# First context attention of a two-layer Perceiver block: where the softmax is divided by its sums

## Chip, cores and metric

The kernel runs on one core of a Trainium2 chip. The metric is device time in microseconds. The kernel before took 872.7 us (median of 3 runs, 870.73 to 873.6).

## The reference, cut to what matters

The whole program is a stack of attention, recurrence and feed-forward parts on x of 16 batches, 64 rows each, width 256. The change is in its first part, cross attention from the normalised rows to a context of 256 rows a batch, with 16 heads of 16 columns:

```
v = (values @ Wv.T).reshape(N, -1, H, D)
k = (keys @ Wk.T).reshape(N, -1, H, D)
q = (queries @ Wq.T).reshape(N, -1, H, D)
energy = jnp.einsum('nqhd,nkhd->nhqk', q, k)
attn = jax.nn.softmax(energy / jnp.sqrt(jnp.float32(E)), axis=3)
out = jnp.einsum('nhql,nlhd->nqhd', attn, v).reshape(N, -1, H * D)
return out @ Wo.T + bo
```

values and keys are both the context ctx_1024. The result is added to x.

## The kernel before, in words

Each stage is a block in which every engine has its own program, in order; engines meet only by semaphores. The first attention is first_attention_stage, about 21 to 166 us of the span. It goes over the 16 batches n. The 16 heads of a batch lie in four banks r = 0 to 3 of PSUM (s_ps), each 128 rows (two heads by 64 queries) by KD = 2 parts by 256 context rows.

For each batch: TensorE makes the scores of all four banks (scores, L1324). VectorE takes the maximum of each bank (maxima, L1479). ScalarE takes the exponential of each bank in two instructions and gets the row sums with them in den (exps, L1417). TensorE turns each bank (transposes, L1333: "turning" below, T(n,r) for bank r) into one of three work banks w_ps that are used in a fixed rotation, written out in the list uses. VectorE copies the turned banks 0 to 2 to probT, ScalarE bank 3 (take_transposed, L1485 and L1424). TensorE multiplies them with the values (values, L1347) into o_ps.

Before, the probabilities are turned undivided. VectorE takes the reciprocals of all sums of the batch (reciprocals, L1491). GpSimd lays them out times a mask (spread_out, L1249), and TensorE multiplies that with a doubled identity (L1353, in values) so that the factors lie as the heads do. At odd n, heads() copies the factors from PSUM (L1495) and multiplies the heads by them (L1499). The output projection of a pair of batches t = n // 2 stands between T(n,1) and T(n,2) of the next even n (output, L1360), and add() adds it to X.

Between these lie the projections for batch n + 3: its keys (keys_of, L1282) after the scores of n + 1, its values (values_of, L1291) after the value product of n. ScalarE takes both to SBUF, the keys between exponentials 1 and 2, the values after exponential 3. For n = 5 and 9 there are also a turning of x and a query projection (query, L1311). GpSimd also makes the query halves (queries, L1239: two instructions for a pair of batches), adds the output bias to X (add_bias) and makes the inverse roots for the next stage's normalisation (following.root, L189 and L193). root at odd n waits for the moments, which VectorE makes in following.find_moments (L122, L184) in its turn of the same n. following.scale_row (L199) on VectorE stands at even n from 4 on.

TensorE's order for one n is written out: four turnings, with the output between T1 and T2 at even n; scores of n + 1; keys of n + 3; value and spreading products of n; values of n + 3. There are no keys or values left to make from n = 13 on.

Of the kernel before, what the change touches and what calls it, by code (L numbers as in the profile page):

```python
# [13 lines left out]
P = 128  # L14
B = 16
# [1104 lines left out]
def first_attention_stage(nc, stage, X, eps, xnT, QT, par_q, half, twice, ident, x_d, ctxT_d, WqT, WkT, WvT, WoT, bo, firsts, constants, others, others_loaded, following):  # L1120
# [14 lines left out]
    with Scope(nc, stage) as sc:  # L1135
# [5 lines left out]
        negmax = [sc.sb(f"negmax{j}", [P, 4, KD]) for j in range(2)]  # L1141
        prob = [sc.sb(f"prob{j}", [P, 4, KD, S]) for j in range(2)]
        probT = [sc.sb(f"probT{j}", [P, 4, KD, 2, P]) for j in range(2)]
        den = [sc.sb(f"den{j}", [P, KD, 4]) for j in range(2)]
        rden = [sc.sb(f"rden{j}", [P, KD, 4]) for j in range(2)]
        spread = [sc.sb(f"spread{j}", [P, KD, 4, 2 * HD]) for j in range(2)]
        factor = sc.sb("factor", [P, 2 * KD, T])
        headsT = sc.sb("headsT", [P, 2 * KD, T])
        s_ps = [sc.ps(f"s_ps{r}", [P, KD, S]) for r in range(4)]
        w_ps = [sc.ps(f"w_ps{i}", [P, 512]) for i in range(3)]  # L1150
        o_ps = sc.ps("o_ps", [P, 2, 2 * KD, T])
        ctx_in = [sc.sem(f"ctx_in{j}") for j in range(NB)]
        (zeroed, k_mm, k_ready, v_mm, v_ready, q_ready, s_mm, max_ready, exp_done, pt_mm, pt_dve, pt_act, pv_mm, rden_ready, spread_ready, factor_ready, heads_ready, out_mm, x_added) = (sc.sem(n) for n in (
            "zeroed", "k_mm", "k_ready", "v_mm", "v_ready", "q_ready", "s_mm", "max_ready", "exp_done", "pt_mm", "pt_dve", "pt_act", "pv_mm",
            "rden_ready", "spread_ready", "factor_ready", "heads_ready", "out_mm", "x_added"))
        turned, turned_taken, query_mm, query_taken, bias_added, constant = (sc.sem(n) for n in ("turned", "turned_taken", "query_mm", "query_taken", "bias_added", "constant"))
        x_in = [sc.sem(f"x_in{g}") for g in range(CH)]
        wk_in, wv_in, turn_in, wq_in, rest_in = (sc.sem(n) for n in ("wk_in", "wv_in", "turn_in", "wq_in", "rest_in"))
        on_act = (3,)
        on_dve = tuple(r for r in range(4) if r not in on_act)  # L1160

        def loaded(n):
# [41 lines left out]
        with sc.block() as block:  # L1204
# [27 lines left out]
            @block.gpsimd  # L1232
            def _(pool):
                def queries(t):
                    pool.wait_ge(query_taken, ONE + t // 2 + 1)
                    if t >= 2:
                        pool.wait_ge(s_mm, ONE + 4 * (2 * t - 2))
                    for e in range(2):
                        nc.gpsimd.tensor_scalar(qpair[t % 2][:, :, :, e, :], QT[:, :, t * P:(t + 1) * P].rearrange("p m (j q) -> p m j q", j=2), par_q[:, e:e + 1], None, ALU.mult).then_inc(q_ready, 1)  # L1239

                def add_bias(t):
                    pool.wait_ge(normed.scaled, ONE + t + 1)
                    nc.gpsimd.tensor_tensor(X[:, t, :], X[:, t, :], bo[:, :], ALU.add).then_inc(bias_added, 1)

                def spread_out(n):
                    pool.wait_ge(rden_ready, ONE + n + 1)
                    if n >= 2:
                        pool.wait_ge(pv_mm, ONE + n - 1)
                    nc.gpsimd.tensor_tensor(spread[n % 2][:, :, :, :].rearrange("p m r d -> p (m r) d"), rden[n % 2][:, :, :].rearrange("p m r -> p (m r)").unsqueeze(2).to_broadcast([P, 4 * KD, 2 * HD]),  # L1249
                                            half[:, :].unsqueeze(1).to_broadcast([P, 4 * KD, 2 * HD]), ALU.mult).then_inc(spread_ready, 1)  # L1250

                following.prepare(pool)
                for j in range(AHEAD):
                    nc.gpsimd.memset(vals[j][:, :, :, :, :], 0.0).then_inc(zeroed, 1)
                pool.wait_ge(rest_in, ONE + 16 * len(firsts["rest"]))
                queries(0)
                queries(1)
                for n in range(B):
                    if n % 2 == 0:
                        if 2 <= n // 2 + 1 < NT:  # L1260
                            queries(n // 2 + 1)
                        add_bias(n // 2)
                    spread_out(n)
                    if n % 2 == 1 and n >= 3:
                        following.root(pool, n // 2 - 1, n // 2)

            @block.tensor
            def _(pe):
# [58 lines left out]

                def transposes(n, r):
                    acc = work_bank((n, r))
                    pe.wait_ge(exp_done, ONE + 4 * n + r + 1)  # L1330
                    for m in range(KD):
                        for c in range(2):
                            mm = nc.tensor.transpose(acc[:, (2 * m + c) * P:(2 * m + c + 1) * P], prob[n % 2][:, r, m, c * P:(c + 1) * P], ident[:, :])  # L1333
                    mm.then_inc(pt_mm, 1)

                def values(n):
                    t, j = n // 2, n % 2
                    pe.wait_ge(v_ready, ONE + 2 * n + 2)
                    if j == 0 and t >= 1:
                        pe.wait_ge(heads_ready, ONE + t)  # L1340
                    for r in (2, 3):
                        pe.wait_ge(*transposed(n, r))
                    for m in range(KD):
                        for e in range(2):
                            for c in range(2):
                                for r in range(4):
                                    nc.tensor.matmul(o_ps[32 * r:32 * r + 32, 0, 2 * m + j, :], vals[n % AHEAD][:, e, c, 4 * m + r, :],  # L1347
                                                     probT[n % 2][:, r, m, c, e * T:(e + 1) * T], start=(e == c == 0), stop=(e == c == 1))
                    if n == 0:
                        pe.wait_ge(rest_in, ONE + 16 * len(firsts["rest"]))  # L1350
                    pe.wait_ge(spread_ready, ONE + n + 1)
                    for m in range(KD):
                        mm = nc.tensor.matmul(o_ps[:, 1, 2 * m + j, :], spread[n % 2][:, m, :, :], twice[:, :], start=True, stop=True)  # L1353
                    mm.then_inc(pv_mm, 1)

                def output(t):
                    pe.wait_ge(heads_ready, ONE + t + 1)
                    acc = work_bank(("out", t))
                    for k in range(KD):
# [13 lines left out]
                for n in range(B):  # L1373
                    ahead = TURNED_BESIDE.get(n)
                    for r in range(4):
# [4 lines left out]
                            query(1)  # L1380
                        if r == 1 and ahead is not None:
                            turn(ahead)
                    if n + 1 < B:
                        scores(n + 1)
                    if ahead is not None:
                        query(ahead)
                    if n + AHEAD < B:
# [7 lines left out]
            def _(act):  # L1395
# [16 lines left out]
                def exps(n, r):  # L1412
# [1 line left out]
                    if n >= 2:  # L1414
                        act.wait_ge(pt_mm, ONE + 4 * (n - 2) + r + 1)
                    for m in range(KD):
                        ins = nc.scalar.activation(prob[n % 2][:, r, m, :], s_ps[r][:, m, :], ACT.Exp, bias=negmax[n % 2][:, r, m:m + 1], accum_out=den[n % 2][:, m, r:r + 1])  # L1417
                    ins.then_inc(exp_done, 1)

                def take_transposed(n, r):  # L1420
# [53 lines left out]
            def _(dve):  # L1474
# [9 lines left out]
                        dve.wait_ge(pv_mm, ONE + n - 1)  # L1484
                    nc.vector.tensor_copy(probT[n % 2][:, r, :, :, :], bank((n, r))[:, :].rearrange("p (m c q) -> p m c q", m=KD, c=2)).then_inc(pt_dve, 1)  # L1485

                def reciprocals(n):
                    dve.wait_ge(exp_done, ONE + 4 * n + 4)
                    if n >= 2:
                        dve.wait_ge(spread_ready, ONE + n - 1)  # L1490
                    nc.vector.reciprocal(rden[n % 2][:, :, :], den[n % 2][:, :, :]).then_inc(rden_ready, 1)  # L1491

                def heads(t):
                    dve.wait_ge(pv_mm, ONE + 2 * t + 2)
                    nc.vector.tensor_copy(factor[:, :, :], o_ps[:, 1, :, :]).then_inc(factor_ready, 1)  # L1495
                    dve.wait_ge(factor_ready, ONE + t + 1)
                    if t >= 1:
                        dve.wait_ge(out_mm, ONE + t)
                    nc.vector.tensor_tensor(headsT[:, :, :], o_ps[:, 0, :, :], factor[:, :, :], ALU.mult).then_inc(heads_ready, 1)  # L1499

                def add(t):
                    dve.wait_ge(out_mm, ONE + t + 1)
# [18 lines left out]
                normed.scale(dve, NT - 1)  # L1521
                for r in range(4):
                    maxima(0, r)
                for n in range(B):
                    for r in range(4):
                        if r == 3:
                            reciprocals(n)
                        if r not in on_act:
                            take_transposed(n, r)
                        if r == 2 and n % 2 == 0 and n > 0:  # L1530
                            add(n // 2 - 1)
                    if n + 1 < B:
                        for r in range(4):
                            maxima(n + 1, r)
                    if n % 2 == 1 and n >= 3:
                        dve.wait_ge(x_added, ONE + n // 2)
                        following.find_moments(dve, n // 2 - 1)
                    if n % 2 == 1:
                        heads(n // 2)
                    if n % 2 == 0 and n >= 4:  # L1540
                        following.scale_row(dve, n // 2 - 2)
                add(NT - 1)


# [1638 lines left out]
```

## Time and profile before

| | us |
|---|---|
| median of 3 runs | 872.7 |
| profiled execution, its own time | 875.52 |
| its span | 873.7 |
| TensorE busy in the span | 754.0 (86%) |
| VectorE busy | 564.5 (65%) |
| ScalarE busy | 416.0 (48%) |
| GpSimd busy | 328.6 (38%) |
| mean granted clock of TensorE | 0.936 of full |

PE is TensorE's matmul, PEld its weight load, DVE is VectorE, ACT ScalarE, POOL GpSimd. Times in the rows are us from the start of the span. The span is somewhat shorter than the execution's own time.

### The profile page before, as it was taken

The page shows a single profiled execution, that of the slowest core. Times are in us where ns is not written, and L with a number is a line of the kernel's source. Part 1 is how long each engine was busy: PE and PEld are TensorE (multiplying, and loading weights), DVE is VectorE, ACT ScalarE, POOL GpSimd, SP SyncE. Part 2 cuts the span into 40 slices and gives each one's busy share as a digit, 9 for nine tenths or more (in the row PEclk, how much of TensorE's full clock was granted, in tenths as well). Part 3 has the DMA queues.
Part 4 walks back from the last instruction along what each step waited for, and adds up shares of the span by engine and source line. Part 5 has one row for each costly group of instructions (what it writes and reads, how often), then busy time and mean ns, then how long its engine had stood idle before and what let it go on. Part 6 is the DMA issues. An engine that isn't in the chain of part 4 may idle for free. (4 is left out here: it accounts for less than half of the span.)

```text
span 873.7 us, 19103 instructions
## 1 busy us (share of the span) xinstructions
PE 754.0 (86%) x7000; PEld 504.6 (58%) x7000; DVE 564.5 (65%) x1234; ACT 416.0 (48%) x1253; POOL 328.6 (38%) x424
## 2 busy tenths in 40 slices
PE   6999999798899999968787399999378888868996
PEld 5788887544333333345465388888257776456334
DVE  3565556536799999976797433232478887567474
ACT  3755656462655665235463100000267884645572
POOL 2222222127477887731253450100554553334001
PEclk9999999998799999988998599999679999979999
DMA  8111710000020000000001046542456420000001
GB/s 268 37 42 54 266 26 2 2 1 1 24 74 1 1 1 1 0 2 0 2 3 50 25 138 192 175 158 73 132 170 194 124 75 2 1 3 3 0 1 50
DMA packets 44893, 51.79 MB, mean 59 GB/s; under 512 B 7072, under 2 KB 40832, under 8 KB 44544
## 3 DMA queue, kind: packets, MB, share of 16 engines
q1 hardware_dynamic: 40256, 43.48, 16.0%
q0 software_dynamic: 1536, 4.20, 1.6%
q10 hardware_dynamic: 3008, 2.88, 0.9%
q8 instruction: 57, 0.93, 0.4%
q14 instruction: 36, 0.29, 0.1%
HBM read 45.31 MB, written 5.24 MB: 58 GB/s over the span
## 5 line engine op out<-in xcount | busy, mean ns | idle before, releaser
L1008 PE MATMUL r_u_ps<-r_t_in,l_same_head 128*128 128x512 f32 x124 | 69.6, 643 | 1.1
L1807 ACT ACTIVATE a_prob<-a_s_ps,a_negmax 128x256 f32<-128x256 f32 x128 | 58.7, 482 | 22.3 <-DVE a_negmax L1843 21.7
L976 POOL TENSOR_TENSOR r_q_in<-r_state,rec_q 128x512 f32<-128x512 f32 x62 | 68.1, 1098 | 0.0
L1417 ACT ACTIVATE a_prob<-a_s_ps,a_negmax 128x256 f32<-128x256 f32 x128 | 59.1, 487 | 17.8 <-DVE a_negmax L1479 17.8
L2436 PE MATMUL m_h_ps<-m_rowsT,l_w 128*128 128x256 f32 x256 | 57.8, 386 | 0.0
L1485 DVE COPY a_probT<-a_w_ps 128x512 f32<-128x512 f32 x48 | 31.4, 687 | 37.2 <-PE a_w_ps L1333 37.0
L2447 PE MATMUL m_y_ps<-l_w,m_hidden 128*128 128x256 f32 x240 | 53.9, 379 | 0.0
L2436 PEld LDWEIGHTS m_h_ps<-m_rowsT,l_w 128*128 128x128 f32 x256 | 49.7, 195 | 7.0
L1843 DVE TENSOR_REDUCE a_negmax<-a_s_ps 128x2 f32<-128x512 f32 x64 | 41.3, 684 | 18.4 <-PE a_s_ps L1723 14.0
L966 POOL TENSOR_TENSOR r_faded<-r_state,rec_both 128x256 f32<-128x256 f32 x62 | 39.8, 642 | 33.5 <-DVE r_state L945 33.5
L2479 ACT ACTIVATE m_rowsT<-m_xt_ps,l_B_s,l_B_g 128x256 f32<-128x256 f32 x16 | 8.2, 559 | 92.4 <-PE m_xt_ps L2424 85.7
L2341 DVE TENSOR_SCALAR m_hidden<-m_h_ps,l_b 128x256 f32<-128x256 f32 x64 | 28.0, 480 | 36.9 <-PE m_h_ps L2436 36.1
L1479 DVE TENSOR_REDUCE a_negmax<-a_s_ps 128x2 f32<-128x512 f32 x64 | 39.8, 684 | 16.2 <-PE a_s_ps L1324 16.2
L2447 PEld LDWEIGHTS m_y_ps<-l_w,m_hidden 128*128 128x128 f32 x240 | 45.1, 190 | 5.9
L936 DVE TENSOR_TENSOR r_update<-r_u_ps,rec_k 128x512 f32<-128x512 f32 x64 | 44.3, 693 | 1.6 <-PE r_u_ps L1002 1.5
L932 DVE TENSOR_TENSOR r_t_in<-r_state,r_par_ps 128x512 f32<-128x512 f32 x62 | 42.6, 687 | 3.2
L2080 POOL TENSOR_TENSOR a_prob<-a_prob,a_rden 128x512 f32<-128x512 f32 x32 | 32.3, 1041 | 30.6 <-DVE a_rden L2149 30.6
L1249 POOL TENSOR_TENSOR a_spread<-a_rden,all_half 128x256 f32<-128x256 f32 x16 | 9.8, 614 | 89.2 <-DVE a_rden L1491 89.2
L1732 PE MATMUL a_w_ps<-all_ident,a_prob 128*128 128x128 f32 x256 | 38.9, 299 | 3.9 <-DVE a_probT L1849 1.7
L1282 PE MATMUL a_w_ps<-a_ctxT,l_A_WkT 128*128 128x256 f32 x128 | 33.4, 406 | 7.1 <-DMA l_A_WkT<-in_A_WkT 6.2
L2365 POOL DMA_INDIRECT m_rows<-routed_rows,m_token x16 | 15.5, 967 | 63.5 <-PE m_xt_ps L2424 42.7
L1732 PEld LDWEIGHTS a_w_ps<-all_ident,a_prob 128*128 128x128 f32 x256 | 31.5, 155 | 12.3 <-issue 7.9
(404 smaller groups left out, 1861.7 us busy)
## 6 DMA issues: line engine op xcount, KB each, us to landing
l_w<-in_B_w SPq DMA_DIRECT2D x16, 1024.0 KB, 5.8
a_ctxT<-in_ctxT SPq DMA_DIRECT2D x31, 256.0 KB, 2.9
a_ctx<-in_ctx SPq DMA_DIRECT2D x16, 256.0 KB, 2.8
expert_out<-m_y ACTq DMA_DIRECT2D x7, 256.0 KB, 5.7
all_X<-in_x SPq DMA_DIRECT2D x4, 256.0 KB, 5.5
l_b<-in_B_b SPq DMA_DIRECT2D x1, 1024.0 KB, 6.0
own_rows<-n_rows SPq DMA_DIRECT2D x2, 512.0 KB, 3.0
all_xnT<-own_rows SPq DMA_DIRECT2D x1, 1024.0 KB, 5.3
```

What stands on the lines that cost most here:

```text
L932: nc.vector.tensor_tensor(t_in[m][:, :, :, :], twice(state[n % 2][m]), a, ALU.mult).then_inc(t_ready[m], 1)
L936: nc.vector.tensor_tensor(update[m][:, :, :, :], u_ps[m][:, :, :, :], steps("k", 2 * n, 2, m), ALU.mult).then_inc(upd_ready[m], 1)
L966: nc.gpsimd.tensor_tensor(faded[m][:, :, :], state[n % 2][m][:, :, :], f, ALU.mult).then_inc(faded_ready[m], 1)
L976: ins = nc.gpsimd.tensor_tensor(q_in[i % 2][m][:, :, :, :], twice(state[i % 2][m]), steps("q", 2 * i - 1, 2, m), ALU.mult)
L1008: nc.tensor.matmul(u_ps[m][:, :, :, :], same_head[:, :], t_in[m][:, :, :, :], start=False, stop=True).then_inc(u_mm[m], 1)
L1417: ins = nc.scalar.activation(prob[n % 2][:, r, m, :], s_ps[r][:, m, :], ACT.Exp, bias=negmax[n % 2][:, r, m:m + 1], accum_out=den[n % 2][: ...
L1479: nc.vector.tensor_reduce(negmax[n % 2][:, r, :], s_ps[r][:, :, :], AX.X, ALU.max, negate=True).then_inc(max_ready, 1)
L1732: mm = nc.tensor.transpose(acc[:, (2 * m + c) * P:(2 * m + c + 1) * P], prob[n % 2][:, r, m, c * P:(c + 1) * P], ident[:, :])
L1807: ins = nc.scalar.activation(prob[n % 2][:, r, m, :], s_ps[r][:, m, :], ACT.Exp, bias=negmax[n % 2][:, r, m:m + 1], accum_out=den[n % 2][: ...
L1843: nc.vector.tensor_reduce(negmax[n % 2][:, r, :], s_ps[r][:, :, :], AX.X, ALU.max, negate=True).then_inc(max_ready, 1)
L2436: mm = nc.tensor.matmul(h_ps[i][:, f, :], w1[j][:, k, (2 * i + f) * P:(2 * i + f + 1) * P], rowsT[j][:, k, :], start=(k == 0), stop=(k == ...
L2447: mm = nc.tensor.matmul(y_bank(e, slice(c, c + 1))[:, 0, :], hidden[j][:, f, c * P:(c + 1) * P], w2[j][:, f, :], start=(f == 0), stop=(f = ...
```

## The change

The probabilities are divided before they are turned. GpSimd multiplies each bank of prob, in place, by the reciprocals of its row sums (normalise, four instructions a batch); the turnings wait for that in place of the exponential. The spreading on GpSimd, the spreading product on TensorE, and the factor copy and product in heads() are dropped; heads() is one copy. VectorE takes the reciprocals bank by bank. TensorE's scores of n + 1 move ahead of T(n,3). ScalarE now copies turned bank 2, VectorE 0, 1 and 3. VectorE's order is written anew.

```diff
-        on_act = (3,)
+        on_act = (2,)
...
-                def spread_out(n):
-                    pool.wait_ge(rden_ready, ONE + n + 1)
...
+                def normalise(n, r):
+                    pool.wait_ge(rden_ready, ONE + 4 * n + r + 1)
+                    nc.gpsimd.tensor_tensor(prob[n % 2][:, r, :, :], prob[n % 2][:, r, :, :], rden[n % 2][:, r, :].unsqueeze(2).to_broadcast([P, KD, S]), ALU.mult).then_inc(prob_ready, 1)
...
                 for n in range(B):
+                    for r in range(4):
+                        normalise(n, r)
                     if n % 2 == 0:
                         if 2 <= n // 2 + 1 < NT:
                             queries(n // 2 + 1)
                         add_bias(n // 2)
-                    spread_out(n)
                     if n % 2 == 1 and n >= 3:
                         following.root(pool, n // 2 - 1, n // 2)
...
                 def transposes(n, r):
                     acc = work_bank((n, r))
-                    pe.wait_ge(exp_done, ONE + 4 * n + r + 1)
+                    pe.wait_ge(prob_ready, ONE + 4 * n + r + 1)
...
-                    pe.wait_ge(spread_ready, ONE + n + 1)
-                    for m in range(KD):
-                        mm = nc.tensor.matmul(o_ps[:, 1, 2 * m + j, :], spread[n % 2][:, m, :, :], twice[:, :], start=True, stop=True)
...
-                    if n + 1 < B:
-                        scores(n + 1)
+                        if r == 2 and n + 1 < B:
+                            scores(n + 1)
...
-                def reciprocals(n):
-                    dve.wait_ge(exp_done, ONE + 4 * n + 4)
+                def reciprocals(n, r):
+                    dve.wait_ge(exp_done, ONE + 4 * n + r + 1)
...
                 def heads(t):
                     dve.wait_ge(pv_mm, ONE + 2 * t + 2)
-                    nc.vector.tensor_copy(factor[:, :, :], o_ps[:, 1, :, :]).then_inc(factor_ready, 1)
-                    dve.wait_ge(factor_ready, ONE + t + 1)
                     if t >= 1:
                         dve.wait_ge(out_mm, ONE + t)
-                    nc.vector.tensor_tensor(headsT[:, :, :], o_ps[:, 0, :, :], factor[:, :, :], ALU.mult).then_inc(heads_ready, 1)
+                    nc.vector.tensor_copy(headsT[:, :, :], o_ps[:, :, :]).then_inc(heads_ready, 1)
...
+                for r in range(4):
+                    reciprocals(0, r)
                 for n in range(B):
...
+                    take_transposed(n, 0)
+                    take_transposed(n, 1)
+                    if n % 2 == 0 and n > 0:
+                        add(n // 2 - 1)
                     if n + 1 < B:
...
+                        maxima(n + 1, 0)
+                        maxima(n + 1, 1)
+                    take_transposed(n, 3)
+                    if n + 1 < B:
+                        reciprocals(n + 1, 0)
+                        maxima(n + 1, 2)
+                        reciprocals(n + 1, 1)
+                        maxima(n + 1, 3)
+                    if n % 2 == 1:
+                        heads(n // 2)
+                    if n + 1 < B:
+                        reciprocals(n + 1, 2)
                     if n % 2 == 1 and n >= 3:
                         dve.wait_ge(x_added, ONE + n // 2)
                         following.find_moments(dve, n // 2 - 1)
-                    if n % 2 == 1:
-                        heads(n // 2)
                     if n % 2 == 0 and n >= 4:
                         following.scale_row(dve, n // 2 - 2)
+                    if n + 1 < B:
+                        reciprocals(n + 1, 3)
```

## Rows read from the trace of the kernel before

**Rows 1.** Busy time by stretch: engine busy us, granted clock, DMA share, GB/s
```profile
29.73:148.10 118.37, 117.99 (x1557) 96.37 (x1556) 70.07 (x138) 73.62 (x264) 26.81 (x41) 1.00 0.24 76
```

**Rows 2.** Timeline, TensorE, 84 to 94 us: start, length, instructions
```profile
84.78 1.15 PE L1324 MATMUL a_s_ps<-a_keysT,a_qpair 32*128 32x256 f32 x16
...
87.78 1.10 PE L1347 MATMUL a_o_ps<-a_probT,a_vals 128*32 128x64 f32 x64
88.81 0.66 PE L1353 MATMUL a_o_ps<-all_twice,a_spread 128*128 128x64 f32 x4
89.30 1.95 PE L1291 MATMUL a_w_ps<-l_A_WvT,a_ctxT 128*128 128x256 f32 x8
91.08 2.04 PE L1333 MATMUL a_w_ps<-all_ident,a_prob 128*128 128x128 f32 x16
93.06 1.15 PE L1324 MATMUL a_s_ps<-a_keysT,a_qpair 32*128 32x256 f32 x16
```

**Rows 3.** Timeline, TensorE, the scores one frame later
```profile
102.27 1.15 PE L1324 MATMUL a_s_ps<-a_keysT,a_qpair 32*128 32x256 f32 x16
```

**Rows 4.** Timeline, ScalarE, same frame: sum reads that end each bank's exponential
```profile
87.49 0.20 ACT L1417 ACTIVATION_READ_ACCUMULATOR a_prob<-a_s_ps,a_negmax 128x1 f32 x1
...
88.38 0.21 ACT L1417 ACTIVATION_READ_ACCUMULATOR a_prob<-a_s_ps,a_negmax 128x1 f32 x1
...
89.76 0.24 ACT L1417 ACTIVATION_READ_ACCUMULATOR a_prob<-a_s_ps,a_negmax 128x1 f32 x1
...
90.66 0.25 ACT L1417 ACTIVATION_READ_ACCUMULATOR a_prob<-a_s_ps,a_negmax 128x1 f32 x1
```

**Rows 5.** Timeline, VectorE, same frame: the four maxima
```profile
85.94 2.49 DVE L1479 TENSOR_REDUCE a_negmax<-a_s_ps 128x2 f32<-128x512 f32 x4 [0.36 <-PE a_s_ps L1324]
```

**Rows 6.** Timeline, VectorE, the moments for the next stage at n = 7
```profile
96.62 0.42 DVE L122 BATCH_NORM_STATS2 n_x_parts<-all_X 128x6 f32<-128x256 f32 x1
97.07 0.18 DVE L184 BATCH_NORM_AGGREGATE n_x_meanvar<-n_x_parts 128x2 f32<-128x6 f32 x1
```

**Rows 7.** Timeline, GpSimd, root at n = 7 and the queries behind it
```profile
97.33 0.19 POOL L189 TENSOR_TENSOR n_x_std<-n_x_meanvar,all_eps 128x1 f32<-128x1 f32 x1 [2.92 <-DVE n_x_meanvar L184]
...
98.16 1.83 POOL L1239 TENSOR_SCALAR a_qpair<-all_QT,all_par 128x256 f32<-128x256 f32 x2
```

**Rows 8.** Timeline, a later attention: reciprocal, normalising, turning
```profile
436.35 0.19 DVE L2149 RECIPROCAL a_rden<-a_den 128x8 f32<-128x8 f32 x1
...
436.63 4.04 POOL L2080 TENSOR_TENSOR a_prob<-a_prob,a_rden 128x512 f32<-128x512 f32 x4 [1.92 <-DVE a_rden L2149]
...
437.72 3.75 PE L2034 MATMUL a_pt_ps<-all_ident,a_prob 128*128 128x128 f32 x16 [0.40 <-POOL a_prob L2080]
```

**Rows 9.** Timeline, TensorE, the frame with a query projection
```profile
73.60 1.15 PE L1324 MATMUL a_s_ps<-a_keysT,a_qpair 32*128 32x256 f32 x16
74.94 1.97 PE L1311 MATMUL a_w_ps<-all_xnT,l_A_WqT 128*128 128x256 f32 x8 [0.19 <-ACT all_xnT L1428]
```

**Rows 10.** Timeline, TensorE, batch 0: T(0,1) and the scores of batch 1
```profile
26.47 0.63 PE L1333 MATMUL a_w_ps<-all_ident,a_prob 128*128 128x128 f32 x4 [0.88 <-ACT a_prob L1417]
...
29.73 1.15 PE L1324 MATMUL a_s_ps<-a_keysT,a_qpair 32*128 32x256 f32 x16
```

**Rows 11.** Timeline, the last batches: scores of 14 and 15, last heads
```profile
148.10 1.15 PE L1324 MATMUL a_s_ps<-a_keysT,a_qpair 32*128 32x256 f32 x16
...
155.06 1.15 PE L1324 MATMUL a_s_ps<-a_keysT,a_qpair 32*128 32x256 f32 x16
...
164.44 0.42 DVE L1499 TENSOR_TENSOR a_headsT<-a_o_ps,a_factor 128x256 f32<-128x256 f32 x1
```

**Rows 12.** Scaling of rows (min/median/max ns, all of the line), and two of them beside GpSimd
```profile
L142 DVE TENSOR_SCALAR a_x_rows<-all_X,a_x_meanvar,a_x_rstd x8: 383/410/1115, 7.8 to 13.6; 128x256 f32<-128x256 f32 x8
...
9.82 1.87 DVE L142 TENSOR_SCALAR a_x_rows<-all_X,a_x_meanvar,a_x_rstd 128x256 f32<-128x256 f32 x2
...
8.67 2.87 POOL L1254 MEMSET a_vals<- 128x1024 f32 x3
```

More of the change, by code:

```diff
@@ L1143, in first_attention_stage @@
         probT = [sc.sb(f"probT{j}", [P, 4, KD, 2, P]) for j in range(2)]
[L1144 to L1147, printed above, removed]
+        den = [sc.sb(f"den{j}", [P, 4, KD]) for j in range(2)]
+        rden = [sc.sb(f"rden{j}", [P, 4, KD]) for j in range(2)]
         headsT = sc.sb("headsT", [P, 2 * KD, T])
@@ L1150, in first_attention_stage @@
         w_ps = [sc.ps(f"w_ps{i}", [P, 512]) for i in range(3)]
-        o_ps = sc.ps("o_ps", [P, 2, 2 * KD, T])
+        o_ps = sc.ps("o_ps", [P, 2 * KD, T])
         ctx_in = [sc.sem(f"ctx_in{j}") for j in range(NB)]
-        (zeroed, k_mm, k_ready, v_mm, v_ready, q_ready, s_mm, max_ready, exp_done, pt_mm, pt_dve, pt_act, pv_mm, rden_ready, spread_ready, factor_ready, heads_ready, out_mm, x_added) = (sc.sem(n) for n in (
+        (zeroed, k_mm, k_ready, v_mm, v_ready, q_ready, s_mm, max_ready, exp_done, pt_mm, pt_dve, pt_act, pv_mm, rden_ready, prob_ready, heads_ready, out_mm, x_added) = (sc.sem(n) for n in (
             "zeroed", "k_mm", "k_ready", "v_mm", "v_ready", "q_ready", "s_mm", "max_ready", "exp_done", "pt_mm", "pt_dve", "pt_act", "pv_mm",
-            "rden_ready", "spread_ready", "factor_ready", "heads_ready", "out_mm", "x_added"))
+            "rden_ready", "prob_ready", "heads_ready", "out_mm", "x_added"))
         turned, turned_taken, query_mm, query_taken, bias_added, constant = (sc.sem(n) for n in ("turned", "turned_taken", "query_mm", "query_taken", "bias_added", "constant"))
@@ L1243, in add_bias @@
                     nc.gpsimd.tensor_tensor(X[:, t, :], X[:, t, :], bo[:, :], ALU.add).then_inc(bias_added, 1)
-                def spread_out(n):
-                    pool.wait_ge(rden_ready, ONE + n + 1)
[L1247 to L1250, printed above, removed]
+                def normalise(n, r):
+                    pool.wait_ge(rden_ready, ONE + 4 * n + r + 1)
+                    nc.gpsimd.tensor_tensor(prob[n % 2][:, r, :, :], prob[n % 2][:, r, :, :], rden[n % 2][:, r, :].unsqueeze(2).to_broadcast([P, KD, S]), ALU.mult).then_inc(prob_ready, 1)
                 following.prepare(pool)
@@ L1346, in values @@
                                 for r in range(4):
-                                    nc.tensor.matmul(o_ps[32 * r:32 * r + 32, 0, 2 * m + j, :], vals[n % AHEAD][:, e, c, 4 * m + r, :],
+                                    mm = nc.tensor.matmul(o_ps[32 * r:32 * r + 32, 2 * m + j, :], vals[n % AHEAD][:, e, c, 4 * m + r, :],
                                                      probT[n % 2][:, r, m, c, e * T:(e + 1) * T], start=(e == c == 0), stop=(e == c == 1))
-                    if n == 0:
-                        pe.wait_ge(rest_in, ONE + 16 * len(firsts["rest"]))
-                    pe.wait_ge(spread_ready, ONE + n + 1)
-                    for m in range(KD):
-                        mm = nc.tensor.matmul(o_ps[:, 1, 2 * m + j, :], spread[n % 2][:, m, :, :], twice[:, :], start=True, stop=True)
                     mm.then_inc(pv_mm, 1)
                 def output(t):
+                    if t == 0:
+                        pe.wait_ge(rest_in, ONE + 16 * len(firsts["rest"]))
                     pe.wait_ge(heads_ready, ONE + t + 1)
@@ L1416, in exps @@
                     for m in range(KD):
-                        ins = nc.scalar.activation(prob[n % 2][:, r, m, :], s_ps[r][:, m, :], ACT.Exp, bias=negmax[n % 2][:, r, m:m + 1], accum_out=den[n % 2][:, m, r:r + 1])
+                        ins = nc.scalar.activation(prob[n % 2][:, r, m, :], s_ps[r][:, m, :], ACT.Exp, bias=negmax[n % 2][:, r, m:m + 1], accum_out=den[n % 2][:, r, m:m + 1])
                     ins.then_inc(exp_done, 1)
@@ L1485, in take_transposed @@
                     nc.vector.tensor_copy(probT[n % 2][:, r, :, :, :], bank((n, r))[:, :].rearrange("p (m c q) -> p m c q", m=KD, c=2)).then_inc(pt_dve, 1)
-                def reciprocals(n):
-                    dve.wait_ge(exp_done, ONE + 4 * n + 4)
+                def reciprocals(n, r):
+                    dve.wait_ge(exp_done, ONE + 4 * n + r + 1)
                     if n >= 2:
-                        dve.wait_ge(spread_ready, ONE + n - 1)
-                    nc.vector.reciprocal(rden[n % 2][:, :, :], den[n % 2][:, :, :]).then_inc(rden_ready, 1)
+                        dve.wait_ge(prob_ready, ONE + 4 * (n - 2) + r + 1)
+                    nc.vector.reciprocal(rden[n % 2][:, r, :], den[n % 2][:, r, :]).then_inc(rden_ready, 1)
                 def heads(t):
                     dve.wait_ge(pv_mm, ONE + 2 * t + 2)
-                    nc.vector.tensor_copy(factor[:, :, :], o_ps[:, 1, :, :]).then_inc(factor_ready, 1)
-                    dve.wait_ge(factor_ready, ONE + t + 1)
                     if t >= 1:
                         dve.wait_ge(out_mm, ONE + t)
-                    nc.vector.tensor_tensor(headsT[:, :, :], o_ps[:, 0, :, :], factor[:, :, :], ALU.mult).then_inc(heads_ready, 1)
+                    nc.vector.tensor_copy(headsT[:, :, :], o_ps[:, :, :]).then_inc(heads_ready, 1)
                 def add(t):
@@ L1523, in _ @@
                     maxima(0, r)
+                for r in range(4):
+                    reciprocals(0, r)
                 for n in range(B):
[L1525 to L1531, printed above, removed]
-                    if n + 1 < B:
-                        for r in range(4):
-                            maxima(n + 1, r)
+                    take_transposed(n, 0)
+                    take_transposed(n, 1)
+                    if n % 2 == 0 and n > 0:
+                        add(n // 2 - 1)
+                    if n + 1 < B:
+                        maxima(n + 1, 0)
[10 more added lines that the diff above has]
+                        reciprocals(n + 1, 2)
                     if n % 2 == 1 and n >= 3:
```

## The prediction

> **What bounds the kernel now.** The table of busy time by stretch comes first. In the 118.37 us from the scores of batch 1 to those of batch 14 TensorE is busy 117.99 us, at a granted clock of 1.00, while VectorE has 70.07, ScalarE 73.62 and GpSimd 26.81 [rows 1]. So in this stretch TensorE's instruction order is the clock of everything, and GpSimd is nearly free. The timeline of TensorE then gives the beat. I call the time from the start of one batch's scores to the start of the next a frame, and give times from its start as +x. A frame without an output projection is 84.78 to 93.06, 8.28 us [rows 2]; one with it is 93.06 to 102.27, 9.21 us [rows 2, 3]. Inside a frame: scores, keys of n+3, value product (+3.00), spreading product (+4.03), values of n+3 (+4.52), the four turnings (+6.30), next scores (+8.28). Third, when the other engines are done with the batch whose scores opened the frame: the four maxima start at +1.16 and take 2.49 [rows 5]; the exponentials of its four banks end at +2.91, +3.81, +5.22 and +6.13 [rows 4].
>
> **What goes.** The spreading product holds TensorE from 88.81 to 89.30: 0.49 us a batch [rows 2]. Since TensorE is the bound, each frame that gets no new wait is 0.49 shorter: 7.79, and 8.72 with output. The GpSimd spreading, the copy of the factors and the product in heads() are off the path in those frames; heads() keeps one copy, 0.42 for this shape [rows 11].
>
> **What comes.** GpSimd normalises 64 tiles of 128x512, in place, between exponential and turning. The stretch of before has no such instruction, the later attention does: four in 4.04, each 1.04 long and 1.00 from the last, the first 0.09 after its reciprocal (436.54 to 436.63), and TensorE starts 0.05 after the first is done (437.67 to 437.72) [rows 8]. Bounds for ours, with two broadcasts of 256 where that has eight of 64: not below a maximum over the same 512 columns on VectorE, 2.49 / 4 = 0.62 [rows 5]; not above 1.83, what GpSimd needs for 2 x 256 columns of the query halves [rows 7]. I take 1.04 and a pace of 1.00, the same operation on the same columns. A reciprocal is 0.19 [rows 8]; the new ones are four a batch, of two numbers.
>
> An even frame (n even, opened by scores n+1) then runs like this. T(n,3) now comes after the scores, so the value product starts at +3.00 + 0.49 = +3.49. The first reciprocal is at about +3.1, GpSimd starts at +3.3 (it may end the queries and the bias of this batch first, so at the latest near +3.7), and tiles are ready at about +4.4, +5.5, +6.5, +7.6. TensorE wants them at +6.30, +6.8, +7.3 and, after the next scores, +8.9. Each is a microsecond or so early: no wait, and the 0.49 stands. Keys and values keep their three banks; what turning waits for there is as far behind it as before.
>
> **An odd frame from n = 3 on is another matter**, and this is the term that decides. At the end of GpSimd's turn for odd n stands following.root(), which waits for moments that VectorE makes in the same turn. GpSimd takes its instructions in order, so normalise(n+1, 0) is queued behind that wait. In the profile root waits already today: 2.92 us, until the aggregate ends at 97.25, then runs 97.33 to 98.16, 0.83 with its second step, and only then come the queries [rows 6, 7]; nothing urgent was behind it. Now VectorE's order puts in front of the moments both heads(), which waits for the value product, and the reciprocal of bank 2, which waits for its exponential:
> - value product +3.49 to +4.6 (1.10 long [rows 2]); heads +4.7 to +5.1;
> - exponential 2 ends +5.22 [rows 4], reciprocal 2 to +5.4;
> - moments 0.63 from first start to last end [rows 6]: +6.03;
> - root +6.12 to +6.95 [rows 7]; tile 0 to +7.98, so T(n+1,0) at +8.03 and T(n+1,1) at +9.03, against +6.30 wanted;
> - then 0.5, output 0.93, T(n+1,2) 0.5 (its tile is ready by +10.0): next scores at +10.96.
> Against 9.21 before, that is +1.75. Three frames are such (n = 3, 7, 11). For n = 5 and 9 a query projection stands between, which moves keys and value product: the old frame is 73.60 to 84.78 = 11.18, less 9.21 and its own wait of 0.19 is 1.78 [rows 2, 3, 9]. Heads ends at +6.8, reciprocal 2 (its exponential now waits behind the keys, to about +6.8) at +7.05, moments +7.7, root +8.6, T0 +9.7, T1 +10.7, next scores +12.6: +1.44 each.
>
> **The two ends.** Batch 0: T(0,1) started at 26.47 behind its exponential [rows 10]; reciprocal, tile and hand-overs put about 0.3 + 1.04 + 0.05 in front, less the 0.14 it waited anyway: +1.27, and with T(0,3) moved behind the scores (-0.49) the scores of batch 1, 29.73, come 0.8 late. Frame 13 has no keys or values to fill TensorE: before it was 148.10 to 155.06 = 6.96 [rows 11]. Now heads +5.15, reciprocal 2 +5.3, moments +5.93, root +6.85, T0 +7.93, T1 +8.93, output, T2, scores of 15 at +10.85: +3.9. Frame 14: tiles ready at +4.3, 5.4, 6.4, 7.35; T3 ends +8.0, its copy +8.75, value product +9.9, heads done +10.4 against 155.06 to 164.86 = 9.80 [rows 11]: +0.6.
>
> A contention at the same place: scale_row() is SBUF to SBUF on VectorE. Two such instructions took 1.87 us at 9.82, beside GpSimd's fills (8.67 to 11.54), where the median of one is 410 ns and the longest 1115 [rows 12]. With normalising beside it in every even turn, reciprocal 3 can come a tile (1.04) late; tile 3 has 8.9 - 7.6 = 1.3 to spare, so only frame 14 pays, half a tile on average: +0.5. The Trainium skill, page "SBUF — State Buffer", section "SBUF: two separate sides", says VectorE in a 2-port mode and GpSimd hold one port pair by exclusive lock and the loser blocks for the whole instruction. Rows 12 agree. By that rule the price is the one above; without it the sum would be 0.5 less.
>
> **The sum.** Start +0.8; eight free frames (n = 0, 1, 2, 4, 6, 8, 10, 12) 8 x -0.49 = -3.9; n = 3, 7, 11: 3 x 1.75 = +5.25; n = 5, 9: 2 x 1.44 = +2.9; frame 13 +3.9; frame 14 +0.6 and +0.5. Together +10.0. The profiled execution took 875.52 (span 873.7), so its counterpart is 885.5. It stands 2.8 above the median of 872.7, so the forecast is 872.7 + 10.0 = 882.7.
>
> **Rivals.**
> - Faster: GpSimd's root does not hold the tiles up (the moments are there in time), so TensorE stays the bound. The thirteen frames before frame 13 would give 13 x -0.49 = -6.4, start +0.8, frame 13 +0.3 (T0 at +4.4 behind a tile), frame 14 +1.1: -4.2, so 868.5. For it: rows 1 and the slack of the even frames. Against it: root's wait is in the profile, and the new order makes it later, not earlier. Chance 0.07.
> - A shorter tile: at the lower bound of 0.62 a stalled frame has T0 at +7.6, then TensorE runs on, scores at +10.0, 0.95 less in each of six: +4.3, so 877. Chance 0.10.
> - GpSimd becomes the bound: with a tile near 1.83, four are 7.3 and queries come on top, more than a frame of 7.79. Both kinds of frame then follow GpSimd, about 2 us more in each of 16: 30 more, so about 912. Against it: the 1.04 of the same operation [rows 8]. Chance 0.03.
> - That the spreading product does not disappear from TensorE's bound, with its 0.49 refilled by an unseen wait in every frame (each reciprocal's semaphore): eight frames give nothing, +13.9, so 886.6. Chance 0.08.
> The likeliest keeps 0.72, with a range of its own of 879 to 886: half a microsecond of error in each of the six stalls is 3.
>
> **How the numbers follow.** A difference under 0.3% (2.6 us) can't be told from none. Faster takes the first rival, 0.07, and a sliver for errors in the stalls: 0.08. Same is 870.1 to 875.3, which needs the short tile and shorter stalls together: 0.05. Slower holds the rest, 0.87. The range reaches from the short tile, 876, a little beyond the refilled bound, 888; outside stay the faster case, the bound on GpSimd and the far ends of the rest, under 0.2.
>
> **What would show it.** Right: no spreading product; scores to scores 7.8 in even frames; in odd frames from 3 on GpSimd idle until the aggregate of n_x_meanvar, root behind it, TensorE idle some 1.7 before the first turning and 0.5 before the second, released by GpSimd's prob, and about 11.0 from scores to scores; busy share of TensorE down to about nine tenths there. Wrong: GpSimd's root waiting for nothing, or TensorE waiting for a tile in even frames too, or tiles far from 1.04.

## The result: 1.5% slower, and the profile after

The changed kernel took 883.92 us (median of 4, 882.72 to 884.62) against 871.72 for the kernel before, ratio 1.0154 (95% interval 1.0130 to 1.0178). Compared again later, side by side with two repaired kernels, it was 882.02 against 870.35, ratio 1.0133 (1.0101 to 1.0165). That is +11.7 to +12.2, where the forecast was +10.0.

Busy time by stretch, the changed kernel, from the scores of batch 1 to those of batch 14 (columns as in [rows 1]):

```profile
31.30:157.69 126.39, 116.90 (x1506) 93.18 (x1505) 73.10 (x170) 73.78 (x265) 71.86 (x80) 0.96 0.22 71
```

TensorE is busy 1.1 us less than before (116.90 against 117.99), in a stretch that is 8.0 longer, and it is now idle for 9.5 of it. Thirteen spreading products of 0.49 have gone from this stretch, so by itself that should have been 6.4 less; in a second profile of the same kernel (experiment 8) it is 6.1 less, 111.90 at a clock of 1.00. Here the mean clock is 0.96, so something beside idle time was lost. GpSimd went from 26.81 to 71.86.

The timeline of TensorE in the frame n = 7, the changed kernel, shows both losses (the same instructions as [rows 2, 3]):

```profile
96.46 1.15 PE L1320 MATMUL a_s_ps<-a_keysT,a_qpair 32*128 32x256 f32 x16
97.54 0.66 PE L1329 MATMUL a_w_ps<-all_ident,a_prob 128*128 128x128 f32 x4
98.03 1.89 PE L1278 MATMUL a_w_ps<-a_ctxT,l_A_WkT 128*128 128x256 f32 x8
99.85 1.10 PE L1343 MATMUL a_o_ps<-a_probT,a_vals 128*32 128x64 f32 x64
100.88 1.99 PE L1287 MATMUL a_w_ps<-l_A_WvT,a_ctxT 128*128 128x256 f32 x8
104.49 0.63 PE L1329 MATMUL a_w_ps<-all_ident,a_prob 128*128 128x128 f32 x4 [1.61 <-POOL a_prob L1245]
105.49 1.09 PE L1329 MATMUL a_w_ps<-all_ident,a_prob 128*128 128x128 f32 x4 [0.37 <-POOL a_prob L1245]
106.37 1.91 PE L1353 MATMUL a_w_ps<-l_A_WoT,a_headsT 128*128 128x256 f32 x4
108.07 1.01 PE L1329 MATMUL a_w_ps<-all_ident,a_prob 128*128 128x128 f32 x4
```

Up to the values of n + 3 every step is within 0.1 of where the forecast put it (value product +3.39, forecast +3.49). Then TensorE is idle 1.61 before the first turning and 0.37 before the second, both released by GpSimd's prob. The second turning, the output projection and the third turning are slow: the output takes 1.91, where the kernel before has, in the same frame:

```profile
100.37 1.10 PE L1360 MATMUL a_w_ps<-l_A_WoT,a_headsT 128*128 128x256 f32 x4
```

The same frame of the changed kernel on GpSimd and VectorE (timelines) gives the cause of the idle time:

```profile
99.43 0.15 DVE L1484 RECIPROCAL a_rden<-a_den 128x2 f32<-128x2 f32 x1
...
101.02 0.42 DVE L1490 COPY a_headsT<-a_o_ps 128x256 f32<-128x256 f32 x1
101.71 0.17 DVE L1484 RECIPROCAL a_rden<-a_den 128x2 f32<-128x2 f32 x1 [0.27 <-ACT a_prob L1410]
101.80 0.41 DVE L122 BATCH_NORM_STATS2 n_x_parts<-all_X 128x6 f32<-128x256 f32 x1
102.24 0.18 DVE L184 BATCH_NORM_AGGREGATE n_x_meanvar<-n_x_parts 128x2 f32<-128x6 f32 x1
```

```profile
102.50 0.19 POOL L189 TENSOR_TENSOR n_x_std<-n_x_meanvar,all_eps 128x1 f32<-128x1 f32 x1 [6.16 <-DVE n_x_meanvar L184]
102.77 0.57 POOL L193 TENSOR_TENSOR n_x_rstd<-n_x_std,n_x_minus_half 128x1 f32<-128x1 f32 x1
103.30 4.03 POOL L1245 TENSOR_TENSOR a_prob<-a_prob,a_rden 128x512 f32<-128x512 f32 x4
107.31 1.83 POOL L1237 TENSOR_SCALAR a_qpair<-all_QT,all_par 128x256 f32<-128x256 f32 x2
```

GpSimd stood 6.16 us in root, while the first reciprocal of the new batch was there from 99.58 (99.43 + 0.15) on. The moments ended at +5.96 of the frame (forecast +6.03), the first tile started at +6.84 (forecast +6.95). Granted clock over the slow products, the changed kernel:

```profile
106.37:108.07 1.70, 1.70 (x5) 1.24 (x5) 0.69 (x1) 0.00 (x0) 1.70 (x2) 0.50 1.03 399
```

0.50 is the lower of the two levels, 1.2 GHz. GpSimd and VectorE worked beside the output projection in the kernel before as well (at 100.37, GpSimd's bias from 99.95 to 100.67 and VectorE's copies from 100.00 to 101.29), at a clock of 1.00.

From scores to scores, us (before: two profiles that agree within 0.02; the changed kernel: the profile above, and a second one of the same kernel, the eighth experiment below):

| frame | before | forecast | profile shown | second profile |
|---|---|---|---|---|
| scores 0 to scores 1 | 8.08 | 8.9 | 10.54 | 8.87 |
| n = 0, 2, 6, 10, 12 | 8.28 | 7.79 | 7.75 | 7.75 |
| n = 4, 8 (8.88 before, a turning of x more) | 8.88 | 8.39 | 8.23 | 8.23 |
| n = 1 | 9.21 | 8.72 | 8.73 | 8.72 |
| n = 3, 7, 11 | 9.21 | 10.96 | 12.55 | 10.90 |
| n = 5, 9 | 11.18 | 12.6 | 12.40 | 12.40 |
| n = 13 | 6.96 | 10.85 | 12.21 | 12.22 |
| sum, scores 0 to scores 15 | 133.4 | 142.3 | 149.14 | 142.53 |

### The profile page after: what moved, and what is told of

The parts are those of the page before. It is cut to its first block and busy times, and to the rows that moved or that the text cites. A ratio compares the mean times of both kernels' runs of the same rounds, so it can differ in the third digit from the quotient of the medians.

```text
span 881.9 us, 19089 instructions
## 1 busy us (share of the span) xinstructions
PE 753.3 (85%) x6936; PEld 501.4 (57%) x6936; DVE 567.9 (64%) x1274; ACT 415.4 (47%) x1253; POOL 384.7 (44%) x472
## 5 line engine op out<-in xcount | busy, mean ns | idle before, releaser
L1245 POOL TENSOR_TENSOR a_prob<-a_prob,a_rden 128x512 f32<-128x512 f32 x64 | 65.4, 1047 | 27.6 <-DVE a_rden L1484 27.5
L1472 DVE TENSOR_REDUCE a_negmax<-a_s_ps 128x2 f32<-128x512 f32 x64 | 42.1, 682 | 27.4 <-PE a_s_ps L1320 27.4
L1329 PE MATMUL a_w_ps<-all_ident,a_prob 128*128 128x128 f32 x256 | 42.4, 301 | 16.1 <-POOL a_prob L1245 16.0
L1843 DVE TENSOR_REDUCE a_negmax<-a_s_ps 128x2 f32<-128x512 f32 x64 | 40.9, 681 | 11.9 <-PE a_s_ps L1723 11.9
L2080 POOL TENSOR_TENSOR a_prob<-a_prob,a_rden 128x512 f32<-128x512 f32 x32 | 32.3, 1042 | 31.4 <-DVE a_rden L2149 31.4
L1732 PE MATMUL a_w_ps<-all_ident,a_prob 128*128 128x128 f32 x256 | 38.4, 295 | 3.7 <-ACT a_prob L1807 2.4
```

Of the source, the lines that this page charges most:

```text
L1245: nc.gpsimd.tensor_tensor(prob[n % 2][:, r, :, :], prob[n % 2][:, r, :, :], rden[n % 2][:, r, :].unsqueeze(2).to_broadcast([P, KD, S]), AL ...
L1472: nc.vector.tensor_reduce(negmax[n % 2][:, r, :], s_ps[r][:, :, :], AX.X, ALU.max, negate=True).then_inc(max_ready, 1)
L1843: nc.vector.tensor_reduce(negmax[n % 2][:, r, :], s_ps[r][:, :, :], AX.X, ALU.max, negate=True).then_inc(max_ready, 1)
```

## The experiments

**1. Root later.** Only GpSimd's order is changed:

```diff
                     for r in range(4):
                         normalise(n, r)
+                    if n % 2 == 0 and n >= 4:
+                        following.root(pool, n // 2 - 2, n // 2 - 1)
...
-                    if n % 2 == 1 and n >= 3:
-                        following.root(pool, n // 2 - 1, n // 2)
+                following.root(pool, NT - 2, NT - 1)
```

> The changed kernel with one edit: GpSimd's root for the moments of turn n (odd) stands behind the four normalisings of n + 1, so no tile waits for the moments. Theory (the root in GpSimd's queue holds the tiles, and TensorE's slow products after the idle time follow from it): frames n = 3, 7, 11 go from 12.55 to about 8.75, n = 5 and 9 from 12.4 to about 10.7, frame 13 from 12.2 to about 7.5; together -19, so about 865. Rival (the normalising itself, its four hand-overs a batch, is what costs): frames stay within 1 us of the changed kernel, about 880 to 884.

Measured 863.99 against 869.29 for the kernel before: ratio 0.9935 (0.9914 to 0.9956), so it is faster than the kernel before and the changed kernel. Frames n = 3, 7, 11: 8.72; n = 5, 9: 10.45; 13: 7.25. The timeline of GpSimd, n = 3 to 4, has normalising first and root behind it:

```profile
58.74 2.04 POOL L1245 TENSOR_TENSOR a_prob<-a_prob,a_rden 128x512 f32<-128x512 f32 x2 [3.42 <-DVE a_rden L1485]
61.03 2.04 POOL L1245 TENSOR_TENSOR a_prob<-a_prob,a_rden 128x512 f32<-128x512 f32 x2 [0.26 <-DVE a_rden L1485]
63.03 0.19 POOL L189 TENSOR_TENSOR n_x_std<-n_x_meanvar,all_eps 128x1 f32<-128x1 f32 x1
```

The root's place in the queue is the cause. Normalising on GpSimd by itself costs the full frames nothing; the first and last ones keep a little (8.9 or 10.5 for 8.08, 7.25 for 6.96, and 10.5 for 9.8 from the last scores to the last heads).

**2. Moments first.** VectorE's find_moments moved ahead of heads() and reciprocal 2, a smaller dose of the same.

```diff
+                    if n % 2 == 1 and n >= 3:
+                        dve.wait_ge(x_added, ONE + n // 2)
+                        following.find_moments(dve, n // 2 - 1)
                     if n % 2 == 1:
                         heads(n // 2)
```

> The changed kernel with VectorE's moments moved ahead of heads() and of reciprocal 2, behind maximum 3; root stays where it is on GpSimd. Theory: the aggregate ends 0.75 earlier (+5.3 in place of +6.0), tile 0 as well, so TensorE's idle time before the first turning at n = 4, 8, 12 shrinks from 1.6 to about 0.9; with the granted clock falling as before that is 6 x -0.75 = -4.5, about 879.5; if it no longer falls at the shorter gap, another -1.3 in each of n = 3, 7, 11, about 875. Rival (the normalising itself costs): 884, no change.

Measured 874.9 (ratio 1.0051, 1.0027 to 1.0075), the lower of the two expected times. Timelines of GpSimd and TensorE, n = 3:

```profile
60.79 0.19 POOL L189 TENSOR_TENSOR n_x_std<-n_x_meanvar,all_eps 128x1 f32<-128x1 f32 x1 [5.47 <-DVE n_x_meanvar L184]
```

```profile
62.79 0.63 PE L1329 MATMUL a_w_ps<-all_ident,a_prob 128*128 128x128 f32 x4 [0.84 <-POOL a_prob L1245]
63.79 0.63 PE L1329 MATMUL a_w_ps<-all_ident,a_prob 128*128 128x128 f32 x4 [0.37 <-POOL a_prob L1245]
64.25 1.03 PE L1353 MATMUL a_w_ps<-l_A_WoT,a_headsT 128*128 128x256 f32 x4
```

Root starts 0.77 earlier and the idle time falls from 1.62 to 0.84, as expected; the output is back at 1.03, the frame 10.1. So in these frames what the moments gain is given back one for one (10.90 without the lower clock, less 0.78, is 10.12). At n = 5 and 9 the stall went altogether (10.45), more than the 0.75 expected. There heads() waits for a value product that comes a query projection later, so that the moments gain 2.3 by no longer standing behind it (they end at +5.17 of the frame n = 5, in the changed kernel at +7.47), and the idle time was only 1.41.

**3. Filler.** The stall stays; TensorE gets unread products (ident by WoT, 128x256, into a score bank already read) before the first turning of n = 4, 8, 12 and 14.

```diff
+                    if n in (4, 8, 12, 14):
+                        pe.wait_ge(exp_done, ONE + 4 * n + 1)
+                        for i in range(7 if n == 14 else 4):
+                            nc.tensor.matmul(s_ps[0][:, 0, :], ident[:, :], WoT[:, 0, :], start=True, stop=True)
```

> The changed kernel with the stall left in, but TensorE given products that nobody reads (128x256, four at n = 4, 8, 12 and seven at n = 14) ahead of the first turning. Theory (TensorE's granted clock falls to the lower level after the idle time, and the output projection and the third turning pay for it): frames n = 3, 7, 11 go from 12.55 to about 11.1 and frame 13 from 12.2 to about 11, together -5.4, about 878.5, with 4 output matmuls in 0.94 again in place of 1.9. Rival (those products are slow because GpSimd or VectorE is in their way): the frames stay at 12.5 or grow, 884 or more.

Median 880.65 (ratio 1.0131, 1.0104 to 1.0159): in time it can't be told from the changed kernel. In the profile the frames are 10.9 and frame 13 is 10.49. Timeline of TensorE, n = 3, whose scores start at 55.48 (55.53 in the changed kernel's first profile, frames within 0.05 until then):

```profile
61.73 1.89 PE L1371 MATMUL a_s_ps<-l_A_WoT,all_ident 128*128 128x256 f32 x8
63.53 0.63 PE L1329 MATMUL a_w_ps<-all_ident,a_prob 128*128 128x128 f32 x4
64.52 0.63 PE L1329 MATMUL a_w_ps<-all_ident,a_prob 128*128 128x128 f32 x4 [0.37 <-POOL a_prob L1245]
64.99 1.03 PE L1353 MATMUL a_w_ps<-l_A_WoT,a_headsT 128*128 128x256 f32 x4
```

GpSimd and VectorE are as busy as before, and the output takes 1.03: they were not in its way. Frame 13 is the firm part. In both profiles of the changed kernel, and in experiment 2, its output projection took 1.8 to 1.9 (experiment 8 has the lines); with the gap filled it takes 1.03 and the frame 1.7 less, 10.49 for 12.21:

```profile
161.78 1.03 PE L1353 MATMUL a_w_ps<-l_A_WoT,a_headsT 128*128 128x256 f32 x4
```

For n = 3, 7 and 11 this is one profile, and experiment 8 below shows what that is worth.

**4. No spreading.** The removed part alone, on the kernel before: no reciprocals, no spread_out, no spreading product, heads copied undivided.

```diff
-                    spread_out(n)
...
-                    pe.wait_ge(spread_ready, ONE + n + 1)
-                    for m in range(KD):
-                        mm = nc.tensor.matmul(o_ps[:, 1, 2 * m + j, :], spread[n % 2][:, m, :, :], twice[:, :], start=True, stop=True)
```

> The kernel before without the spreading on GpSimd, the spreading product, the reciprocals and the factors; the heads are copied undivided, so the division by the sums is left out of the first attention. It gives the price of the removed part alone. Theory (TensorE is the bound): 0.49 less in each of 13 frames and about 0.5 to 1 in the last two, -7.2, about 864.5. Rival (another wait takes the 0.49 up): 871 to 872.

Measured 862.95 (ratio 0.9913, 0.9881 to 0.9946). Timeline of TensorE; the values of n + 3 now follow the value product directly:

```profile
45.47 1.15 PE L1323 MATMUL a_s_ps<-a_keysT,a_qpair 32*128 32x256 f32 x16
...
48.47 1.10 PE L1346 MATMUL a_o_ps<-a_probT,a_vals 128*32 128x64 f32 x64
49.50 1.99 PE L1290 MATMUL a_w_ps<-l_A_WvT,a_ctxT 128*128 128x256 f32 x8
51.33 2.04 PE L1332 MATMUL a_w_ps<-all_ident,a_prob 128*128 128x128 f32 x16
53.30 1.15 PE L1323 MATMUL a_s_ps<-a_keysT,a_qpair 32*128 32x256 f32 x16
```

53.30 - 45.47 = 7.83 against 8.28: 0.45 a frame, nearly the whole 0.49. TensorE was the bound.

**5 and 10. Batch 0 mended.** Experiment 1 with reciprocal 0 between the maxima, and three unread products ahead of the first turning.

```diff
+                    if n == 0:
+                        pe.wait_ge(exp_done, ONE + 1)
+                        pe.wait_ge(rest_in, ONE + 16 * len(firsts["rest"]))
+                        for i in range(3):
+                            nc.tensor.matmul(s_ps[0][:, 0, :], ident[:, :], WoT[:, 0, :], start=True, stop=True)
```

> The kernel of the first experiment (root behind the next normalisings) with batch 0 mended too: reciprocal 0 between the maxima, and three unread products of 128x256 on TensorE ahead of the first turning, so that it isn't idle there. Theory (in batch 0 TensorE idles 1.5 us for the first tile and then makes the query projection at the lower clock, 3.2 us in place of 1.9): scores 0 to scores 1 go from 10.54 to about 9, the query projection to 1.9, so 1.5 less, about 862.5. Rival (the query projection is late for another reason): 10.5 stays, 864.

The profile gave 8.87 for 10.54 in batch 0, as the theory wants. But the time was 866.03, ratio 0.9935 (0.9910 to 0.9960), no better than experiment 1, so it was run again beside it:

> Root later and batch 0 mended, again. From scores 0 to scores 15 it took 127.12 against 128.81. Theory (the first attention's end moves the whole program): 1.7 less than the run before it. Rival (1.7 disappears in what follows, where the clock or a load decides): no difference.

864.71 and 864.17, ratios 0.9940 (0.9922 to 0.9958) and 0.9938: no difference. The next experiment says why.

**9. Root later, again.**

> Root behind the next normalisings, again, to compare with the next run on the same chip. Expected 0.65% below the kernel before, 865.

Timeline of TensorE, batch 0, this second profile of experiment 1:

```profile
26.64 0.63 PE L1330 MATMUL a_w_ps<-all_ident,a_prob 128*128 128x128 f32 x4 [1.48 <-POOL a_prob L1245]
27.80 0.63 PE L1330 MATMUL a_w_ps<-all_ident,a_prob 128*128 128x128 f32 x4 [0.53 <-POOL a_prob L1245]
28.26 1.89 PE L1308 MATMUL a_w_ps<-all_xnT,l_A_WqT 128*128 128x256 f32 x8
```

Its first profile had the same idle times, 1.48 and 0.53, and then 3.38 for this query projection; here it is 1.89, without any filler. So the 8.87 of experiment 5 does not show the filler at work: whether the clock falls after these gaps differs from one execution to the next. The theory of experiment 5 is left without support. The time doesn't follow such a difference either: from scores 0 to the last heads this profile of experiment 1 is 1.7 us shorter than the first (137.64 and 139.32) and its execution 4.6 us shorter (863.03 and 867.67), so the other 2.9 lie elsewhere in the program.

**8. The changed kernel, again.**

> The changed kernel, unchanged, beside the two repaired ones on one chip. The profile of before that was shown had 7 us in the second context attention that a second profile didn't have, so the change's own price should come out at the difference of the first attention: 149.14 from scores 0 to scores 15 against 133.41, 15.7, and about 0.9 in the last batch, +16 (ratio 1.018). Rival (the 12.2 of the first comparison is the size): ratio 1.014.

Ratio 1.0133: the rival's size. Timeline of TensorE, frame n = 3:

```profile
62.79 0.63 PE L1329 MATMUL a_w_ps<-all_ident,a_prob 128*128 128x128 f32 x4 [1.63 <-POOL a_prob L1245]
63.79 0.63 PE L1329 MATMUL a_w_ps<-all_ident,a_prob 128*128 128x128 f32 x4 [0.37 <-POOL a_prob L1245]
64.25 1.03 PE L1353 MATMUL a_w_ps<-l_A_WoT,a_headsT 128*128 128x256 f32 x4
```

The same idle 1.63, and the output at 1.03. In frame 13 the clock fell here too, and it was still low in scores 15, which take 1.93 for 1.15:

```profile
159.60 2.08 PE L1329 MATMUL a_w_ps<-all_ident,a_prob 128*128 128x128 f32 x8 [3.35 <-POOL a_prob L1245]
161.48 1.91 PE L1353 MATMUL a_w_ps<-l_A_WoT,a_headsT 128*128 128x256 f32 x4
...
164.18 1.93 PE L1320 MATMUL a_s_ps<-a_keysT,a_qpair 32*128 32x256 f32 x16
```

In this execution the first attention is 142.53 from first to last scores, 9.1 over before; in the other 15.7. To the last heads it is 153.83 and 159.85, against 143.21 before: 10.6 and 16.6 over. The times of the two executions do not show this: 883.74 and 883.69. At the last heads this one stands 5.1 us ahead (175.48 against 180.61 on the trace), and at the end of the span it is level (882.0 and 881.9); of that lead 1.5 went in attention_inputs_stage (27.1 for 25.6), 1.4 in moe_stage (144.2 for 142.8) and 1.7 in latent_inputs_stage (21.5 for 19.8, at a mean clock of 0.92 for 1.00). The kernel is the same in both.

**6. Scores behind.** Experiment 1 with the scores back behind the fourth turning.

```diff
-                        if r == 2 and n + 1 < B:
-                            scores(n + 1)
+                    if n + 1 < B:
+                        scores(n + 1)
```

> The kernel of the first experiment with the scores of n + 1 back behind the fourth turning. It asks what moving the scores ahead is worth by itself. Tile 3 was ready at about +7.6 of a frame, and TensorE would want it at +7.25 (+8.2 with an output), so by the forecast's arithmetic 0.3 to 0.5 is lost in frames without output and nothing in those with one: 7 x 0.4 = +3, about 867, with waits for prob before the fourth turning. Rival (VectorE's new order makes everything later in turn, since its copy of bank 3 and the maxima follow): 8 us or more, 872. Other rival: no loss, 864.

Measured 870.61, ratio 0.9997 (0.9977 to 1.0016): the whole gain gone, about twice what I expected, and nearer the 872 of the rival, by which VectorE's new order makes everything later. Timeline of TensorE:

```profile
55.01 2.25 PE L1330 MATMUL a_w_ps<-all_ident,a_prob 128*128 128x128 f32 x16
57.20 1.15 PE L1321 MATMUL a_s_ps<-a_keysT,a_qpair 32*128 32x256 f32 x16
```

The turnings take 57.20 - 55.01 = 2.19 against 1.98 [rows 2], and the value product, behind VectorE's copy of bank 3, comes 0.2 later as well: frames 8.25 and 8.96 for 7.75 and 8.73. The frame from 14 to 15 takes 8.54 for 7.25; its value product, after 2.05 us idle, ran at a granted clock of 0.50 (1.94 for 1.10). My arithmetic had the tile's wait and not the copy's, nor the last batches and their clock. So experiment 1 gains only with the scores ahead: what the removed part gives (6.3 in experiment 4) is taken back without them.

**7. The kernel before, again.**

> The kernel before, unchanged, for a second profile. In the profile shown, its second context attention has two frames of 10.0 us (scores 0 to 1 and 2 to 3) that take 6.9 and 5.8 in the changed kernel, whose code there is the same. Theory (that differs from run to run and isn't the change's doing): frames of 6.9 and about 5.8 to 6.7 this time, the stage 93 from first to last scores, and a time of about 869. Rival (the changed kernel gains there): 99.6 again and about 875.

Measured 871.44; its second context attention took 92.77 between first and last scores, frames 6.93 and 5.76. The 99.58 of the profile shown was that execution's own, not a gain of the change.

## Why the prediction was right, and where its sizes were off

- The spreading product's 0.49 a free frame: right. Even frames are 7.75 for 7.79, and experiment 4 has it alone.
- The tile: 1.04 at a pace of 1.00 was taken over from another attention; 64 of them have a median of 1.039. The bounds of 0.62 and 1.83 were not needed.
- Root's place, the deciding term: shown by taking it away (experiment 1) and by a smaller dose (2). Stalled frames 10.90 for 10.96 and 12.40 for 12.6, where the clock stayed up in them (experiment 8).
- The sum in that execution: 142.53 - 133.4 = +9.1 to the last scores (forecast 142.3), and from there to the last heads 11.3 for 9.8, +1.5 (forecast +1.1). That is +10.6 for a forecast of +10.0, and it comes so near in part by luck: frame 13 was 1.4 dearer and the last frame 0.4, while n = 5 and 9 (-0.4), n = 4 and 8 (-0.3) and some hundredths in each other frame made up for most of it.
- Batch 0: the terms as written add up to 1.25 and not to 1.27, which leaves +0.8; measured +0.8 where the clock stayed up (8.87 for 8.08).
- What was missing: a term for the clock. Every idle time was priced as idle time, none by what follows it. In the profile shown it costs 1.65 in each of n = 3, 7, 11 and 1.67 in batch 0, and in both profiles 1.7 in frame 13 (12.21 against the 10.49 of experiment 3). So frame 13 (+5.25 for +3.9) is the mis-sized term: its stall came out 0.4 smaller than forecast, and the clock put 1.7 on top.
- The 1.7 to 2.2 by which the median exceeds the forecast stay open. The first attention costs +10.6 in one execution and +16.6 in the other, but the two took the same time. From the last heads to the end of the span, four profiles differ by up to 7.5 us (the kernel before 708.8 and 705.7, the changed kernel 701.3 and 706.5), and the forecast has no term for that. So the nearness of its total, 882.7 for a measured 883.9, does not by itself confirm the sum; the frames do.
- scale_row() beside the normalising, +0.5: not seen. In the even turns from n = 4 to 12 it starts just behind a tile (at n = 6: tile to 93.95, scale_row from 94.04, the next tile from 94.21) and takes 0.40; only in the last frame does it meet a running tile:

```profile
174.98 0.51 DVE L199 TENSOR_SCALAR n_rows<-all_X,n_x_meanvar,n_x_rstd 128x256 f32<-128x256 f32 x1
```

That tile ran from 174.30 to 175.34, so 0.36 of it was left, and scale_row took 0.11 longer. Where the clock was up, the last frame took 10.51 to its heads (six of the experiments), and the forecast had 10.4 without this term. The rule on the shared port pair, from the Trainium skill's "SBUF — State Buffer", section "SBUF: two separate sides", had its example in [rows 12]; this trace does not bear it out in full, as far as GpSimd's spans can be trusted to a tenth: by the rule scale_row would have lost the 0.36, and it lost 0.11. So the 0.5 worked out by it was too much.
- Not tried alone: VectorE's new order and the move of one copy between VectorE and ScalarE. The expected gain of 0.49 a frame came with them in place, so they cost the full frames nothing that shows.

## What to carry to other kernels

When urgent work is put on an engine that so far had slack, read what waits in its queue ahead of it: a wait that cost nothing while nothing urgent stood behind it becomes the path. Compare the two orders turn by turn; here one call moved by one turn made +1.5% into -0.6%. Price an idle gap on TensorE twice, once as idle and once with what follows at half the clock. Take two profiles before a difference of a frame is put down to an edit, and look at the whole program's time before a gain of one stage is counted: here 5 us between two executions of one kernel were gone by the end.

## What the hardware showed unexpectedly

After the same idle 1.6 us TensorE went on at a granted clock of 0.50 in one execution of the changed kernel and at 1.00 in another; after 1.48 and 0.53 in batch 0 likewise (3.38 and 1.89 for the query projection, two executions of experiment 1). With these idle times in batch 0 it fell in all five executions whose scores 0 began at 20.76 us and in neither of the two in which they began at 21.65; that this offset decides was not tested. After 0.84 (experiment 2) and after 1.41 (n = 5, 9) no fall was seen. In frame 13, after 1.46 and then 2.95 to 3.35 with the value product between, it fell in all three executions, and neither with the filler in the gap nor after 1.46 and 0.37 (experiment 1).
